# Weighted expert rows, summed by accumulating gathers inside the expert stage of a transformer block

## The chip, the cores and the metric

The kernel runs on one NeuronCore of a Trainium2 chip. The metric is the device time of one execution in microseconds (us). The engines are PE (TensorE, matrix products), DVE (VectorE), ACT (ScalarE), POOL (GpSimd) and SP (SyncE, here only DMA issue); PEld is PE's loading of stationary operands.

## The reference, cut to what matters

One block for x of 4 sequences x 512 tokens x 512 channels: a gate, causal attention with 16 heads, a second gate, and a mixture of experts. This is the part that the change touches:

```python
scores = sigmoid(x @ gate_w)                    # 2048 tokens, 32 experts
# the best 2 of 4 groups are masked out; top 6 experts of the rest
weights = take_along_axis(scores, selected_experts); weights /= sum(weights)
xs = repeat(x, 6)[argsort(selected_experts)]     # rows in expert order
g, u = ragged_dot(xs, w_gate, sizes), ragged_dot(xs, w_up, sizes)    # 512 -> 352
d = ragged_dot(silu(g) * u, w_down, sizes)                          # 352 -> 512
expert_out = sum(d[unsort].reshape(T, 6, 512) * weights[..., None], axis=1)
shared = silu(x @ sw_gate) * (x @ sw_up) @ sw_down                  # 512 -> 704 -> 512
out = x1 + expert_out + shared        # x1: the stream after attention
```

All products are made in three passes over operands that are split into a high and a low part.

## The kernel before

The program is a row of stages, and between stages all engines meet.

`attention` also routes the first three sequences, `choose` on DVE, and POOL sends their rows: `send` takes a tile of 128 rows (`x_rows`), which SP has loaded, and `send_rows` scatters it six times to the HBM tensor `xs` (`slots_in`), one slot for each chosen expert. POOL's order of work (weight splits "u", query splits "r" and "h", sends "z") is written out by hand in `POOL_ORDER`.

`last_route_and_shared_up` does the same for the last sequence and computes the hidden values of the shared expert, `hsh`, in 24 items (6 parts of the weights by 4 sequences). SP loads the shared weights part by part, and stores a block of zeros behind the rows of each expert (`filled`). POOL scatters the last 24 times. DVE makes a table that gives the expert and the first row for each of 127 blocks. 127 is the most that the routing could need; blocks past the last real one read a row of zeros. The table's first column is also used as PE's index of the weights.

`experts` runs 127 blocks of 128 rows in a software pipeline over all engines. For each block ACT loads the rows (`xg`), PE transposes them, ACT and DVE split them, PE multiplies by the expert's gate and up weights, ACT applies SiLU, DVE multiplies, PE transposes the hidden values, ACT and DVE split these, PE multiplies by the down weights, and ACT evicts the result (`rows_out`) and stores it to `ys` (`slots_out`). POOL splits the weights of the 32 experts into high and low, two buffers, so expert e is split when the last gate and up product of expert e - 2 is done. Its last split is expert 31's. At the end SP loads `xT`, 4 MB, the stream x1 transposed.

`combine` is the last stage. SP loads the shared down weights; ACT and DVE split them. For each of 16 tiles of 128 tokens POOL copies six slot numbers and gathers six tiles of rows from `ys`, PE forms the shared product and adds x1 by a product with the identity, and DVE adds the six gathered tiles, each times its weight, to the PSUM result, one after the other. Buffers are double, so POOL waits for DVE's sum of the tile two before. DVE's low part of `hsh` for the next tile stands behind the sums of this tile on its queue.

Of the kernel before, what the change touches and what calls it, by code (L numbers as in the profile page):

```python
# [14 lines left out]
P = 128  # L15
# [18 lines left out]
CAP = T + P  # L34
ZERO_ROW = E * CAP
# [617 lines left out]
def attention(nc, keep, dr, x, fs, wq, wk, wv, wo, gate_w):  # L653
# [5 lines left out]
    with ExitStack() as ctx:  # L659
# [6 lines left out]
        kin, xin = sb("k_rows", [P, TC, P]), sb("x_rows", [P, TC, P])  # L666
# [12 lines left out]
        xc, xh, fc, rowst, rowt = clst, chst, ex, xst, xin  # L679
# [22 lines left out]
        rows_left = sem("rows_left_T")  # L702
# [44 lines left out]
        def _(sp):  # L747
# [111 lines left out]
            def load_rows(u):  # L859
# [7 lines left out]
                sp.dma_start(rowt[:].rearrange("p t c -> p (t c)"), dr["x2"][P * u:P * (u + 1), :]).then_inc(rows_in, 16)  # L867
# [47 lines left out]
        def _(pool):  # L915
# [33 lines left out]
            def send(u, part):  # L949
# [5 lines left out]
                send_rows(nc, pool, dr, rt, slot, rowt[:].rearrange("p t c -> p (t c)"), u, part, 2)  # L955
# [15 lines left out]
            nc.gpsimd.memset(slot[:], 0).then_inc(consts, 1)  # L971
            nc.gpsimd.memset(rt["gm"][:], -1.0).then_inc(consts, 1)
# [28 lines left out]
        def _(pe):  # L1001
            pe.wait_ge(consts, 11)
# [363 lines left out]
        def _(dve):  # L1366
# [139 lines left out]
            for it in range(-1, NIT):  # L1506
                for e in DVE_START if it < 0 else DVE_ORDER[phase(it)]:
                    kind = e[0]
                    if e[0] == "m":
                        if e[1] in "DP":  # L1510
                            b = choice_of(it)
                            if b is not None:
                                if e == "mD0" and b == 0:
                                    dve.wait_ge(consts, 11)
# [48 lines left out]
def last_route_and_shared_up(nc, keep, dr, sw_gate, sw_up, w_gate, w_up, w_down):  # L1563
# [5 lines left out]
    with ExitStack() as ctx:  # L1569
# [4 lines left out]
        x2, rows = sb("x2_last", [P, KC, S]), sb("rows_last", [P, TC, C])  # L1574
        f2 = keep["early"]
# [9 lines left out]
        zero, ends = sb("zero_rows", [P, C]), sb("region_ends", [1, E], I32)  # L1585
# [25 lines left out]
        def _(sp):  # L1611
# [32 lines left out]
            load_shared(3)  # L1644
            sp.wait_ge(ends_done, 1)
# [7 lines left out]
            sp.wait_ge(filled, 16 * (E + 1))  # L1653
# [3 lines left out]
        def _(pool):  # L1657
# [13 lines left out]
            pool.wait_ge(slot_done, B)  # L1671
            for t in range(TC):
                send_rows(nc, pool, dr, rt, slot, rows[:, t, :], NT - TC + t, 0, 1)

        @block.tensor
        def _(pe):
# [17 lines left out]
            for i, (m, b) in enumerate(items):  # L1694
# [12 lines left out]
                if (m, b) == (2, 1):  # L1707
                    pe.wait_ge(row_done, 1)
                    pe.wait_ge(left, KC)
                    for c in range(2):  # L1710
                        last = nc.tensor.transpose(pst[0][0:1, c * P:(c + 1) * P], tabf[:, c:c + 1], ident[:])
                    last.then_inc(row_mm, 1)

        @block.scalar
        def _(act):
# [29 lines left out]
            act.wait_ge(filled, 16 * (E + 1))  # L1745
            act.wait_ge(h_dve, B * (3 - POOL_ITEMS) + 1)
            act.wait_ge(x2_done, CHUNKS + KC)
            for n in range(2):
                row = act.value_load(xrow[0:1, n:n + 1], min_val=0, max_val=ZERO_ROW)
                act.dma_start(f2[:, n, :], dr["xs"][bass.ds(row, P), :]).then_inc(xg_in[n], 16)  # L1750

        @block.vector
        def _(dve):
# [68 lines left out]
            for i in range(B * POOL_ITEMS, len(items)):  # L1822
# [4 lines left out]
                if (m, b) == (3, 0):  # L1827
                    dve.wait_ge(row_mm, 1)
                    then(nc.vector.tensor_copy(ebi[:, 0, :], pst[0][0:1, 0:P]))
# [17 lines left out]
def experts(nc, keep, dr, w_gate, w_up, w_down):  # L1847


    ident, tab, blocks, xT = (keep[k] for k in ("ident", "tab", "blocks", "xT"))  # L1850
    xrow = keep["rowtab"]
    with ExitStack() as ctx:
# [3 lines left out]
        raw, xg = keep["we_raw"], keep["early"]  # L1856
# [428 lines left out]
```

## Time and profile before

| what | value |
|---|---|
| device time, median of 3 runs | 2552.12 us (2549.28 to 2552.67) |
| the profiled execution, its own time | 2533.66 us |
| its span, first to last instruction | 2531.6 us |
| PE busy in the span | 2253.8 us, 89% |
| POOL busy in the span | 1444.6 us, 57% |
| expert stage | about 1456 to 2366 us |
| last stage | about 2366 to 2531.6 us |

All times inside the kernel are us from the start of the profiled span. "Idle before" is the time that an engine stood still ahead of an instruction, and the arrow names what ended it. A busy PE is not PE at its peak, because matmuls are pipelined.

### The profile page before, as it was taken

How to read it: one execution, taken by the hardware profiler on the slowest of the kernel's cores; microseconds unless marked ns; L12 is line 12 of the kernel's file. 1: busy time of each engine (PE TensorE's matmuls, PEld its weight loads, DVE VectorE, ACT ScalarE, POOL GpSimd, SP SyncE). 2: the span in 40 equal slices, each digit the busy share in tenths (PEclk: the TensorE clock that was granted, in tenths of full speed). 3: DMA queues.
4: the chain of work that ended last, by engine and by line, in shares of the span. 5: the costliest groups of instructions: out<-in, count | busy, mean ns of one | idle time of the engine just before them, and what ended most of it. 6: DMA issues, size and time to landing. Idle time of an engine off the chain costs nothing. (4 is left out here: it accounts for less than half of the span.)

```text
span 2531.6 us, 42000 instructions
## 1 busy us (share of the span) xinstructions
PE 2253.8 (89%) x12059; PEld 1928.7 (76%) x12060; DVE 1264.8 (50%) x2120; ACT 1171.2 (46%) x2505; POOL 1444.6 (57%) x976
## 2 busy tenths in 40 slices
PE   1579999999999989898979989999999799999666
PEld 1458888888877768777768689999988699999544
DVE  6737777777755675767653222222222122222365
ACT  3347677777767767776631123333322132333210
POOL 7647777777754556576634046350669955410376
PEclk6789999999999999999979999999999899999888
DMA  4234444433354455554357045352557655522466
GB/s 122 70 114 129 126 125 150 154 100 121 107 169 155 125 163 160 177 175 141 117 220 266 24 138 181 113 166 86 181 163 226 194 169 181 199 86 78 127 196 188
DMA packets 285671, 372.37 MB, mean 147 GB/s; under 512 B 20213, under 2 KB 187193, under 8 KB 280825
## 3 DMA queue, kind: packets, MB, share of 16 engines
q1 hardware_dynamic: 229112, 251.41, 32.2%
q10 hardware_dynamic: 41088, 69.22, 8.4%
q0 software_dynamic: 15360, 50.34, 6.1%
q8 instruction: 60, 0.98, 0.2%
q14 instruction: 51, 0.41, 0.1%
HBM read 257.66 MB, written 113.25 MB: 147 GB/s over the span
## 5 line engine op out<-in xcount | busy, mean ns | idle before, releaser
L1918 POOL TENSOR_SCALAR we_high<-we_raw 128x1408 fp32r<-128x1408 f32 (+1 forms) x95 | 134.1, 1411 | 396.5 <-PE up_e L649 315.9
L1920 POOL TENSOR_TENSOR we_low<-we_raw,we_high 128x1408 fp32r<-128x1408 f32 (+1 forms) x95 | 314.4, 3309 | 7.9
L2034 DVE TENSOR_TENSOR hT_low<-hT_ps,hT_high 128x256 fp32r<-128x256 f32 x127 | 53.9, 425 | 391.4 <-ACT hT_high L1997 391.4
L2047 DVE TENSOR_TENSOR hidden_e<-silu_e,up_e 128x352 f32<-128x352 f32 x127 | 66.1, 521 | 283.6 <-ACT silu_e L2008 283.6
L2008 ACT ACTIVATE silu_e<-gate_e 128x352 f32<-128x352 f32 x127 | 59.0, 465 | 316.8 <-PE up_e L649 316.8
L649 PE MATMUL gate_e<-we_high,xT_high 128*128 x508 | 177.7, 350 | 20.7 <-POOL we_low L1920 20.2
L2013 ACT ACTIVATE rows_out<-down_e 128x512 f32<-128x512 f32 x127 | 75.9, 598 | 216.0 <-PE down_e L649 216.0
L649 PE MATMUL gate_e<-we_high,xT_low 128*128 x508 | 166.1, 327 | 0.0
L649 PE MATMUL gate_e<-we_low,xT_high 128*128 x508 | 165.7, 326 | 0.0
L649 PE MATMUL up_e<-we_high,xT_high 128*128 x508 | 164.4, 324 | 0.0
L649 PE MATMUL up_e<-we_high,xT_low 128*128 x508 | 163.2, 321 | 0.0
L649 PE MATMUL up_e<-we_low,xT_high 128*128 x508 | 163.1, 321 | 0.0
L649 PE MATMUL down_e<-we_high,hT_high 128*128 x381 | 149.6, 393 | 2.4 <-issue 2.4
L1412 DVE TENSOR_TENSOR pT_low<-weights_T,pT_high 128x512 fp32r<-128x512 f32 (+1 forms) x192 | 108.8, 593 | 84.2 <-ACT pT_high L1244 83.8
L649 PE MATMUL down_e<-we_low,hT_high 128*128 x381 | 150.8, 396 | 0.0
L649 PE MATMUL down_e<-we_high,hT_low 128*128 x381 | 150.5, 395 | 0.0
L1226 ACT ACTIVATE prob<-scores,neg_max 128x128 f32<-128x128 f32 (+3 forms) x256 | 131.6, 528 | 39.5 <-DVE neg_max L1397 39.4
L927 POOL TENSOR_TENSOR q_low<-q_raw,q_high 128x512 fp32r<-128x512 f32 x64 | 111.8, 1754 | 54.4 <-ACT q_high L1209 54.3
L1397 DVE TENSOR_REDUCE neg_max<-scores 128x1 f32<-128x128 f32 (+3 forms) x256 | 110.9, 481 | 63.6 <-PE scores L1054 63.1
L923 POOL TENSOR_TENSOR wK_low<-w_ring,wK_high 128x512 fp32r<-128x512 f32 x64 | 88.4, 1388 | 78.0 <-ACT wK_high L1191 77.9
L923 POOL TENSOR_TENSOR wO_low<-w_ring,wO_high 128x512 fp32r<-128x512 f32 x64 | 92.3, 1445 | 60.3 <-ACT wO_high L1191 60.2
L1235 ACT ACTIVATE prob<-prob,row_inv 128x128 f32<-128x128 f32 (+3 forms) x256 | 122.7, 557 | 7.3 <-DVE row_inv L1405 7.3
(341 smaller groups left out, 7332.4 us busy)
## 6 DMA issues: line engine op xcount, KB each, us to landing
rows_early<-slots_in ACTq DMA_DIRECT2D x129, 256.0 KB, 2.7
slots_out<-rows_out ACTq DMA_DIRECT2D x127, 256.0 KB, 2.1
we_raw<-L_ffn_w_gate SPq DMA_DIRECT2D x32, 704.0 KB, 4.6
we_raw<-L_ffn_w_up SPq DMA_DIRECT2D x32, 704.0 KB, 5.0
q_T<-q_out SPq DMA_DIRECT2D x64, 256.0 KB, 2.5
q_raw<-q_T SPq DMA_DIRECT2D x16, 1024.0 KB, 7.7
w_ring<-L_attn_Wk SPq DMA_DIRECT2D x64, 256.0 KB, 3.1
w_ring<-L_attn_Wv SPq DMA_DIRECT2D x64, 256.0 KB, 4.8
```

What stands on the lines that cost most here:

```text
L649: last = nc.tensor.matmul(out, a, b, start=start and i == 0, stop=stop and i == len(terms) - 1)
L923: tt(w_split(*u, 1), ring[:, i % RING, :], w_split(*u, 0).bitcast(F32), ALU.subtract).then_inc(u_lo, 1)
L927: tt(head(ql, n), head_raw(n), head(qh, n).bitcast(F32), ALU.subtract).then_inc(q_lo, 1)
L1226: last = nc.scalar.activation(prob[:, n % 2, P_AT[i]:P_AT[i] + w], pss[x_][:, at:at + w], ACT.Exp, bias=nmax[:, n % 2, i:i + 1], accum_out ...
L1235: last = nc.scalar.activation(w, w, ACT.Copy, scale=rinv[:, n % 2, i:i + 1])
L1397: last = nc.vector.tensor_reduce(nmax[:, n % 2, i:i + 1], pss[x_][:, at:at + (i + 1) * P], AX.X, ALU.max, negate=True)
L1412: tt(ptl[:, at:at + w], pst[(3 * n + x_) % 2][:, 0:w], pth[:, at:at + w].bitcast(F32), ALU.subtract).then_inc(t_lo, 1)
L1918: nc.gpsimd.tensor_scalar(wh[:, p, at:to], raw[:, at:to], 1.0, 1.0, ALU.mult, ALU.mult).then_inc(w_hi, 1)
L1920: nc.gpsimd.tensor_tensor(wl[:, p, at:to], raw[:, at:to], wh[:, p, at:to].bitcast(F32), ALU.subtract).then_inc(w_split, 1)
L2008: nc.scalar.activation(sg[:], psg[:], ACT.Silu).then_inc(s_done, 1)
L2013: nc.scalar.activation(yb[:, p, :], psy[p][:], ACT.Copy).then_inc(y_ev, 1)
L2047: nc.vector.tensor_tensor(hb[:], sg[:], psu[:], ALU.mult).then_inc(h_done, 1)
```

## The change

Rows in `xs` grow from 512 to 528 numbers (`XW`). The 16 new ones (`meta`) hold the token's eight best weights and its six experts. In the expert stage three small DVE operations pick the weight of a row in its block: the six experts are compared with the block's expert (`ebf`, a new table that PE spreads over all partitions), multiplied by the weights and summed. ACT's eviction multiplies by it, so `ys` holds weighted rows. ACT's load of the next rows moves behind SiLU and waits for DVE's use of the old ones.

When the last expert is split and two blocks past the last real one have been evicted, POOL gathers from `ys` into `acc`, one tile of 128 x 512 for each of 16 token tiles: the first choice by a plain gather, the other five by gathers with `compute_op=ALU.add`. Two pairs of groups of four tiles take turns, and a group's next round waits until its round before has landed. The stage ends when all have. SP fills the 31 blocks of `ys` from block 96 on with zeros in the stage before, and loads the shared down weights behind the last split, where it loaded `xT`. The last stage is written out in full, without loops; SP loads x1's tile, PE's work is as before, with four PSUM banks for two, and DVE has one add a tile.

```diff
+                    nc.gpsimd.tensor_copy(rowt[:, C:XW], keep["meta"][:, u, :]).then_inc(rows_ready, 1)
+                    pool.wait_ge(rows_ready, u + 1)
...
+            sp.dma_start(dr["ys"][NREAL * P:NBLK * P, :].rearrange("(n p) c -> p n c", p=P),
+                         zero[:, 0:C].unsqueeze(1).broadcast_to([P, NBLK - NREAL, C])).then_inc(filled, 16)
...
+                    nc.tensor.matmul(pst[1][:, 0:P], tabf[:, 0:1].broadcast_to([P, P]), ident[:], start=True, stop=True).then_inc(row_mm, 1)
...
-            for b in range(B):
-                sp.dma_start(xT[:, b, :, :], dr["x1"][b].rearrange("p (k s) -> p k s", k=KC)).then_inc(x1_in, 16)
-            sp.wait_ge(x1_in, 16 * B)
+            sp.wait_ge(w_split, len(W_PARTS) * (E + 1) + 1)
+            full, tail = (len(SCH) - 1) * P, SCH[-1][1]
+            sp.dma_start(raw[:, 0:(len(SCH) - 1) * C].rearrange("p (k c) -> p k c", c=C),
+                         sw_down[0:full, :].rearrange("(k p) c -> p k c", p=P)).then_inc(sd_in, 16)
+            sp.dma_start(raw[0:tail, (len(SCH) - 1) * C:len(SCH) * C], sw_down[full:, :]).then_inc(sd_in, 16)
...
+            real = pool.value_load(blocks[0:1, E - 1:E], min_val=NREAL, max_val=NBLK)
+            pool.wait_ge(y_ev, real + (CREDIT + 2))
+            pool.sem_inc(pool_steps, 1)
+            for pair in range(2):
+                for k in range(TOPK):
+                    for g in range(2):
+                        if k:
+                            pool.wait_ge(y_in[g], 16 * TC * (TOPK * pair + k))
+                        for t in range(TC * (2 * pair + g), TC * (2 * pair + g + 1)):
+                            more = dict(compute_op=ALU.add) if k else dict()
+                            pool.indirect_dma_start(acc[:, t, :], None, dr["ys"],
+                                                    bass.IndirectOffsetOnAxis(ap=yslot[:, t, k:k + 1], axis=0), **more).then_inc(y_in[g], 16)
...
-                    nc.scalar.activation(yb[:, p, :], psy[p][:], ACT.Copy).then_inc(y_ev, 1)
+                    nc.scalar.activation(yb[:, p, :], psy[p][:], ACT.Copy, scale=wrow[:, q:q + 1]).then_inc(y_ev, 1)
...
+                    nc.vector.tensor_tensor(match[:], xg[:, p, EAT:EAT + TOPK], ebf[:, bass.ds(n, 1)].broadcast_to([P, TOPK]),
+                                            ALU.is_equal).then_inc(m_steps, 1)
+                    nc.vector.tensor_tensor(mine[:], match[:], xg[:, p, WAT:WAT + TOPK], ALU.mult).then_inc(m_steps, 1)
+                    nc.vector.tensor_reduce(wrow[:, q:q + 1], mine[:], AX.X, ALU.add).then_inc(m_done, 1)
...
+                tt(ob[:, n % 2, :], pso[n % 4][:], acc[:, n, :], ALU.add).then_inc(o_done, 1)
```

## Rows read from the trace of the kernel before

**Rows 1.** The page: span, and shares of the chain that ended last.
```profile
span 2531.6 us, 42000 instructions
...
POOL 3%; issue 2%; DMA 1%; DVE 1%; PE 0%; POOLq 0%; ACT 0%; ACTq 0%; SPq 0%; DVEq 0%
```
**Rows 2.** Windows: stretch, length, busy PE, PEld, DVE, ACT, POOL, PEclk, DMA share, GB/s.
```profile
1500.00:2200.00 700.00, 673.27 (x3938) 616.35 (x3937) 171.37 (x395) 206.19 (x492) 408.11 (x174) 0.99 0.51 162
2271.00:2366.00 95.00, 89.01 (x518) 80.98 (x516) 22.60 (x53) 27.82 (x67) 0.00 (x0) 0.98 0.23 75
2366.00:2531.00 165.00, 101.94 (x416) 78.20 (x416) 91.94 (x146) 25.92 (x50) 107.18 (x112) 0.82 0.64 187
```
**Rows 3.** Waits, last stage: us in total, times, longest.
```profile
POOL slot_tile L2104 <- DVEq L2157: 138.8, 1, 138.8
...
PE out_ps L649 <- DVE h_low L2170: 53.1, 14, 18.9
...
DVE acc L2184 <- DMA expert_rows<-slots_out,slot_tile: 50.4, 14, 6.3
```
**Rows 4.** Groups by line, last stage: busy us, mean ns | idle before.
```profile
L2108 POOL DMA_INDIRECT expert_rows<-slots_out,slot_tile x96 | 103.2, 1076 | 37.4 <-issue 23.2 <-POOL slot_tile L2104 13.1 <-DVE out_rows L2184 1.2
...
L2177 DVE TENSOR_SCALAR wts_tile<-wts 128x8 f32 (+1 forms) x16 | 2.6, 165 | 0.0
```
**Rows 5.** Line 2108, the gathers: time to landing.
```profile
DMA to landing us min/median/max: 3.2/3.8/6.8
```
**Rows 6.** POOL's timeline around 2368 us: start, duration [idle before].
```profile
2367.54 1.06 POOL L2108 DMA_INDIRECT expert_rows<-slots_out,slot_tile  x1 [0.90 <-POOL slot_tile L2104]
2368.91 0.96 POOL L2108 DMA_INDIRECT expert_rows<-slots_out,slot_tile  x1 [0.31 <-issue]
```
**Rows 7.** Line 2013, 2269 to 2366 us: the last evictions of the expert stage.
```profile
L2013 ACT ACTIVATE rows_out<-down_e x15: 597/597/602, 2269.7 to 2363.0; 128x512 f32<-128x512 f32 x15
```
**Rows 8.** Timeline of ACT and PE, start of the last stage.
```profile
2374.41 2.34 ACT L2140 ACTIVATE sd_high<-sd_raw 128x2560 fp32r<-128x2560 f32 x1 [10.81 <-DMA sd_raw<-L_ffn_sw_down]
...
2381.78 0.79 PE L649 MATMUL out_ps<-sd_high,h_high 128*128 128x512 f32 x1 [18.87 <-DVE h_low L2170]
...
2388.89 0.50 PE L649 MATMUL out_ps<-sd_high,h_high 128*128 128x512 f32 x1
...
2394.74 0.50 PE L649 MATMUL out_ps<-sd_high,h_high 128*128 128x512 f32 x1 [0.37 <-DVE h_low L2170]
...
2400.47 0.50 PE L649 MATMUL out_ps<-sd_high,h_high 128*128 128x512 f32 x1 [0.25 <-DVE h_low L2170]
```
**Rows 9.** The page's DMA issues: count, KB each, median us to landing.
```profile
rows_early<-slots_in ACTq DMA_DIRECT2D x129, 256.0 KB, 2.7
...
w_ring<-L_attn_Wk SPq DMA_DIRECT2D x64, 256.0 KB, 3.1
```
**Rows 10.** Timeline, DVE's last instruction.
```profile
2528.21 0.75 DVE L2184 SCALAR_TENSOR_TENSOR out_rows<-expert_rows,wts_tile,acc 128x512 f32<-128x512 f32 x1
```
**Rows 11.** DMA, 2366 to 2531 us: POOL's queue (packets, MB, share of 16 engines).
```profile
q0 software_dynamic: 7680, 25.17, 54.0%
```
**Rows 12.** DMA, 1329 to 1397 us: POOL's queue, 24 scatters.
```profile
q0 software_dynamic: 1920, 6.29, 23.2%
```
**Rows 13.** DMA, 2271 to 2366 us: ACT's queue.
```profile
q10 hardware_dynamic: 3888, 7.08, 23.0%
```
**Rows 14.** DVE's timeline in one expert block.
```profile
2258.70 0.68 DVE L2041 TENSOR_TENSOR xT_low<-xT_ps,xT_high 128x512 fp32r<-128x512 f32 x1
2261.36 0.52 DVE L2047 TENSOR_TENSOR hidden_e<-silu_e,up_e 128x352 f32<-128x352 f32 x1 [1.98 <-ACT silu_e L2008]
```
**Rows 15.** Windows, as in rows 2: the fills and scatters before the experts.
```profile
1347.00:1397.00 50.00, 50.00 (x224) 41.29 (x223) 17.06 (x39) 7.28 (x11) 23.15 (x24) 1.00 0.91 340
```
**Rows 16.** ACT's timeline: the split of part 4 of the shared weights.
```profile
1387.68 1.05 ACT L1721 ACTIVATE sw_high<-sw_raw 128x1024 fp32r<-128x1024 f32 x1
```
**Rows 17.** Windows, as in rows 2: attention with the sends.
```profile
920.00:1296.00 376.00, 334.52 (x1753) 275.83 (x1751) 254.49 (x461) 246.38 (x518) 238.34 (x194) 0.95 0.47 153
```

More of the change, by code:

```diff
@@ L34 @@
 CAP = T + P
+XW = C + 16
+WAT, EAT = C, C + 8
+NREAL = T * TOPK // P
 ZERO_ROW = E * CAP
@@ L1844, with experts @@
 W_PARTS = ((0, W_UP, 1), (W_UP, W_DOWN, 1), (W_DOWN, W_N, 2))
-def experts(nc, keep, dr, w_gate, w_up, w_down):
-    ident, tab, blocks, xT = (keep[k] for k in ("ident", "tab", "blocks", "xT"))
+def experts(nc, keep, dr, w_gate, w_up, w_down, sw_down):
+    ident, tab, blocks, acc, ebf, yslot = (keep[k] for k in ("ident", "tab", "blocks", "acc", "ebf", "yslot"))
     xrow = keep["rowtab"]
@@ L2047, in step, with combine @@
                     nc.vector.tensor_tensor(hb[:], sg[:], psu[:], ALU.mult).then_inc(h_done, 1)
-            pipeline(dve, NBLK, 2, 2, step)
-def combine(nc, keep, dr, sw_down, out):
-    xT, ident, hsh, wts, slot = (keep[k] for k in ("xT", "ident", "hsh", "wts", "yslot"))
+            pipeline(dve, NBLK, 4, 2, step)
+def combine(nc, keep, dr, out):
+    ident, hsh, acc = (keep[k] for k in ("ident", "hsh", "acc"))
     NS = len(SCH)
+    tail = SCH[-1][1]
     with ExitStack() as ctx:
@@ L2072, in combine @@
-        pool_steps, act_steps = keep["pool_steps"], keep["act_steps"]
-        block = ctx.enter_context(nc.Block())
-        tail = SCH[-1][1]
-        def loop(eng, step):
-            with eng.Fori(0, B) as b:
-                for t in range(TC):
-                    step(TC * b + t, t % 2, (TC // 2) * b + t // 2, b, t)
+        xc, ob = sb("x1_tile", [P, 2, KC, P]), sb("out_rows", [P, 2, C])
+        pso = [ctx.enter_context(nc.psum_tensor(f"out_ps{i}", [P, S], F32)) for i in range(4)]
+        w_hi, w_lo, hi, lo = sem("sd_hi"), sem("sd_lo"), sem("h_hi6"), sem("h_lo6")
@@ new lines, in load @@
+            def load(n):
+                if n >= 2:
+                    sp.wait_ge(o_mm, n - 1)
+                b, t = divmod(n, TC)
+                sp.dma_start(xc[:, n % 2, :, :], dr["x1"][b].rearrange("p (k s) -> p k s", k=KC)[:, :, at(t)]).then_inc(x_in[n % 2], 16)
+            load(0)
+            load(1)
+            for n in range(NT):
+                if n + 2 < NT:
+                    load(n + 2)
+                b, t = divmod(n, TC)
+                sp.wait_ge(o_done, n + 1)
+                sp.dma_start(out[b, at(t), :], ob[:, n % 2, :]).then_inc(o_out[n % 2], 16)
@@ L2117, in _ @@
+            for p in range(2):
+                sp.wait_ge(o_out[p], 16 * NT // 2)
         @block.tensor
         def _(pe):
-            pe.sem_inc(o_mm, CREDIT)
             pe.wait_ge(w_lo, 1)
-            def step(n, p, half, b, t):
-                pe.wait_ge(lo, done(n))
-                pe.wait_ge(o_done, done(n - 2))
-                parts = [((hh[0:w, p, c, :], hl[0:w, p, c, :]), (wh[0:w, c, :], wl[0:w, c, :])) for c, (at, w) in enumerate(SCH)]
-                split_products(nc, pso[p][:], parts[:1], True, False)
-                pe.wait_ge(x_c, done(n))
+            for n in range(NT):
+                p, bank = n % 2, pso[n % 4]
+                parts = [((hh[0:w, p, c, :], hl[0:w, p, c, :]), (wh[0:w, c, :], wl[0:w, c, :])) for c, (_, w) in enumerate(SCH)]
+                pe.wait_ge(lo, n + 1)
+                if n >= 4:
+                    pe.wait_ge(o_done, n - 3)
+                split_products(nc, bank[:], parts[:1], True, False)
+                pe.wait_ge(x_in[p], 16 * (n // 2 + 1))
@@ L2191, in build @@
+            tt(wl[0:tail, NS - 1, :], raw[0:tail, NS - 1, :], wh[0:tail, NS - 1, :].bitcast(F32), ALU.subtract).then_inc(w_lo, 1)
+            low(0)
+            for n in range(NT):
+                if n + 1 < NT:
+                    low(n + 1)
+                dve.wait_ge(o_mm, n + 1)
+                if n >= 2:
+                    dve.wait_ge(o_out[n % 2], 16 * (n // 2))
+                tt(ob[:, n % 2, :], pso[n % 4][:], acc[:, n, :], ALU.add).then_inc(o_done, 1)
 def build(nc, x, fs, cond, w1, u1, wq, bq, wk, bk, wv, bv, wo, bo, w2, u2,
```

186 lines of the change are left out of this document (74 added, 112 removed).

## Prediction

> **What bounds the kernel now.** I read the page first [rows 1]: the span is 2531.6 us and the chain of waits that ended last names POOL's gathers first, so the end is the last stage's. The windows [rows 2] split the tail. From 1500 to 2200 us, in the expert blocks, PE is busy for 673 of 700 us; the DMA engines are busy 0.51 of that time. From 2271 to 2366 PE is still 89 of 95 us busy, POOL does nothing and the DMA share falls to 0.23. From 2366 to the end PE is busy 102 of 165 us and POOL 107. So the experts are bound by PE and the last stage is not. The waits of the last stage [rows 3] say by what: DVE waits 50.4 us for gathered rows, and DVE's low parts of the hidden values, queued behind those sums, hold PE for 53.1 us. The gathers are 96, of 1.08 us in the mean [rows 4], and one lands 3.8 us after its issue [rows 5]. In POOL's timeline [rows 6] an undisturbed one is 0.96 us behind 0.3 us of issue. The waits [rows 3] also hold what the change wants to use: after its last weight split POOL waits 138.8 us for the end of the expert stage.
>
> Why that gap is there: the expert stage always runs 127 blocks, and the routing of the reference's inputs, counted out, fills 111 of them (it puts expert 29's last block at number 105). Blocks 111 to 126 read a row of zeros. In the new code POOL may start once 113 blocks have left PSUM, which is block 112's eviction. It is the first of the last 15, at 2269.7 us [rows 7].
>
> The sum is made against the profiled execution (2533.7 us of its own time, 2531.6 us of span). The median of the timed runs is 2552.1 us; I carry the difference in us over to it unchanged. 0.2%, about what a measurement here tells from no change, is 5.1 us.
>
> **The change part by part.**
>
> *The last stage* loses its gathers, its weighting and six sums a tile, and the load of its weights, which SP now makes in the expert stage after the last split (2227 us), long before use. It begins with ACT's split of the weights, as before at 2374.4 [rows 8]. Its first product then started 7.4 us later (2381.78); with 0.3 us for the start of the stage, 7.7 us. The first tile took 7.1 us (2381.78 to 2388.89), partly at a low clock. A tile that hardly waited took 2394.74 to 2400.47 less its 0.25 us of waiting, 5.5 us: that is PE's own time, and 15 such are 82 us. DVE, 91.9 us busy in this stage now [rows 2], loses 96 sums of 0.75 us and keeps one add of that size a tile, (91.9 - 72 + 12) / 16 = 2.0 us a tile; ACT has 25.9 / 16 = 1.6 us. Both are under 5.5. The tile of x now comes by its own load of 256 KB, which can start when the tile two before is done, so it has one tile and three products, 6.2 us; a load of 256 KB in weights' rows landed in 3.1 us [rows 9]. After the last product come 0.3 + 0.75 us for the add and 2.6 us for the store, as the old end shows (last DVE instruction over at 2529.0, span 2531.6) [rows 10]. Sum: 7.7 + 7.1 + 82.2 + 3.7 = 100.7 us, against 165.3 us (2366.3 to 2531.6). **Gain 64.6 us.** If the loads of x take 8 us instead of 3.1, each tile waits 1.8 us and 29 us of this go.
>
> *The expert stage* now ends when the last gather has landed. POOL starts at 2270.3 + 0.9 us (the wait between its copy and the first gather [rows 6]) = 2271.2. The old end is 2366.3, so 95 us are covered. There are 16 plain gathers (k = 0) and 80 adding ones. No row shows an adding gather, so it is bounded from both sides, on three resources.
> - POOL's issue. Floor: the plain 0.96 + 0.30 = 1.26 us. Ceiling: twice the descriptor work, 2 x 0.96 + 0.30 = 2.22 us.
> - The DMA engines. A plain gather takes 54.0% of 165 us / 96 = 0.93 us of all 16 [rows 11]; a scatter of the same rows in a crowded stretch 23.2% of 68 us / 24 = 0.66 us [rows 12]. Adding reads the destination too. If every byte counts alike, three passes for two, that is 1.5 times: 1.0 to 1.4 us. If the read side sets the pace, twice: 1.3 to 1.86 us. The blocks that run beside them take 23.0% of 95 us = 21.9 us in all [rows 13].
> - The chain of rounds. Two groups of four tiles take turns, and a group's next round waits for its last to land. Eight issues are 10.1 us, so a landing under 6.3 us costs nothing; the plain one has 3.8 us [rows 5], and the adding one an extra read.
>
> I take 1.5 times on the middle of 0.66 and 0.93, 1.19 us: the engines need 16 x 0.93 + 80 x 1.19 + 21.9 = 132 us. POOL at the last stage's mean of 1.08 + 0.30 = 1.38 us needs 132 us too. The end is 2271.2 + 132 + 3.8 for the last landing + 0.6 for the change of stage = 2407.6 us, 41.3 us later than now. **Loss 41.3 us.** At the floor (1.26 us) it is 2396.6, a loss of 30.3 us.
>
> The trace's plain gather is bound by POOL's issue (1.26 against 0.93 us), and it says nothing on a second read. The Trainium skill, "Collectives: The Full Stack", section "The bandwidth ceiling: the fold count and why AG ≠ RS ≠ AR", states that a DMA that adds needs two source reads on the same read ring, and gives 1.93 as the measured ratio to a copy. By it the DMA sum would be 14.9 + 80 x 1.80 + 21.9 = 181 us and the stage would end some 49 us later than I take; no run here shows it yet.
>
> *The expert blocks.* Each gets three DVE operations on 6 elements. The nearest row is the 128x8 one, 0.16 us [rows 4]; three with their waits are 0.7 us a block. They stand after the low part of x, which ends at 2259.38, and before the hidden product, which begins at 2261.36 after 1.98 us of idling [rows 14]. Cover is left over; without it the cost would be 127 x 0.7 = 89 us. ACT's load of the next rows moves behind SiLU, which ends where the hidden product begins, so to about 2261.5. PE needs the rows two blocks on, about 8 us later, and such a load lands in 2.7 us [rows 9]. Its 0.35 us of issue fit before the next eviction, for which ACT waits for PE. The scale in the eviction is free, the four 1 MB loads of x are gone. Cost 0; rows of 2112 bytes make these transfers 3% longer, hidden too.
>
> *Ahead of the experts.* The fill of 31 blocks of zeros is 31 x 256 KB = 8.1 MB on SP's queue. It goes in at about 1329 us, when the DMA engines have little to do; at the 340 GB/s of the stretch after it [rows 15] it takes 24 us, 9 of them past 1344, where the first expert's weights and 32 fills queue behind it. These ended about 1400 and are needed at 1453. The shared weights of part 4 land about 1368, and 9 us later is still before ACT splits them (1387.7) [rows 16]. The first experts' weights are needed at 1456. Cost 0; if the fill ran at half that rate, part 4 would be about 15 us late and the cost about 15 us. In attention POOL gets 12 copies of 16 columns and a wait each, 0.2 us of copy and up to the 0.9 us of [rows 6] before the next DMA; POOL is busy 238 of 376 us there [rows 17]. Behind them stand q's and the weights' low parts, on which PE waits in turn. Between 0 and 12 us; I take 1.5. PE's one more product and DVE's copy of it: 0.5 us.
>
> **Sum:** -64.6 + 41.3 + 2 = -21.3 us, so 2531 us on the median.
>
> **The rivals.**
> 1. *Adding doubles the DMA time* (slower). Place: the 80 adding gathers. At 2 x 0.93 = 1.86 us the engines need 14.9 + 148.8 + 21.9 = 185.6 us; with about 1 us for the last to land and 0.6, the stage ends at 2458.4, 92.1 us later, and the kernel is 29.5 us slower, 2582 us. It decides from 1.49 us on (2429 us less 2271.2, 1.6, 14.9 and 21.9, over 80), 1.6 times the plain one. For it: an adding read has to be moved by the same engines. Against it: the same bytes took 0.66 us where the engines were crowded, twice of which is 1.3 us. By the Trainium skill's ratio, above, it would be 25 us slower.
> 2. *Adding doubles POOL's issue* (slower). At 2.22 us POOL needs 20.2 + 177.6 = 197.8 us: 107 us later, 44 us slower, 2596 us. It decides from 1.67 us. Against it: scatters and gathers, unlike in direction, cost POOL the same 0.96 us.
> 3. *POOL's floor holds.* 1.26 us each, nothing else binds: 2552 - 32 = 2520 us.
> 4. *Between:* 1.4 to 1.49 us on the engines; within 0.2% or a little faster, about 2546 us.
> 5. *Adding is far dearer* (a row read, summed and written before the next starts, so that a round's landing rules): three issues and a landing make a round, and ten rounds add. At 10 us a landing that is 20 + 138 us and the kernel some 6 us slower, at 20 us a landing 20 + 238 us and over 100 us slower.
>
> **How the numbers follow.** My forecast 0.34 (2522 to 2540 us); floor 0.12; between 0.16 (0.05 of it faster, 0.11 within 0.2%); doubled DMA time 0.18; doubled issue 0.10; far dearer 0.10. Faster 0.51, same 0.11, slower 0.38. The range from 2518 to 2596 us leaves out a little below the floor and most of the last case, 0.12. The likeliest case's own range is 2522 to 2540 us.
>
> **What the profile after would show.** The last stage about 100 us, PE at 5.5 us a tile, no wait for gathers. POOL's first gather about 1 us behind block 112's eviction, near 2271 us, and 96 gathers in 125 to 140 us. The issue and landing of the adding gathers tell rivals 1, 2 and 5 apart: issues of 1.3 us with waits between rounds and a DMA share near 1 are rival 1; issues of 2 us rival 2; long landings at a low share rival 5. Expert blocks still 6.7 us apart. The forecast is wrong if the adding gather is over 1.49 us, if tiles of the last stage wait for x, or if the stages before 1456 us move by more than 3 us.

## The result and the profile after

The changed kernel takes 2585.97 us in the median (2585.0 to 2594.43, 4 runs), the kernel before 2550.7 us beside it (2548.58 to 2552.67, 4 runs): a ratio of 1.0135, 95% interval 1.0112 to 1.0159. It is slower by 35 us, where I had forecast 21 us faster. One thing is needed to read the profiles: in some executions of either kernel ScalarE stands still for 21 to 25 us near 1380 us. The first profile of before is one without that wait, the first of after one with it, so their spans (2531.6 and 2592.7 us) differ by 61 us and not by 35. The experiments have both kinds of both kernels.

The page of the changed kernel (span; busy slices; chain; POOL's gathers with their busy time, mean ns and idle time before):

```profile
span 2592.7 us, 42124 instructions
...
DVE  6737777777765666757552334343455444432012
...
POOL 7657777777754557566612044442479864528820
...
DMA  4234444444444446543387045443456654449942
...
PE 3%; DVE 0%; ACT 0%; issue 0%
...
L1957 POOL DMA_INDIRECT expert_sums<-slots_out,yslot x96 | 138.7, 1444 | 73.6 <-ACT x_batch L2049 44.1
```

The chain that ended last now runs through PE's products of the last stage alone, where POOL's gathers led before [rows 1]. The gathers stand in slices 36 to 39, as POOL's 2, 8, 8, 2 and DMA's 9, 9 show. In windows (the expert blocks, the gathers, the last stage; columns as in rows 2):

```profile
1483.00:2300.00 817.00, 769.39 (x4472) 703.85 (x4473) 355.07 (x787) 245.00 (x558) 445.69 (x190) 0.98 0.50 157
2316.00:2490.00 174.00, 96.81 (x512) 85.81 (x511) 27.29 (x89) 28.47 (x65) 138.15 (x96) 0.80 0.96 185
2493.00:2592.70 99.70, 88.18 (x416) 67.01 (x416) 30.64 (x50) 17.65 (x34) 0.00 (x0) 0.95 0.26 85
```

The last stage takes 99.1 us from ACT's first instruction, and PE is busy 88 of them, against 102 of 165 before [rows 2]. But the stretch ahead of it, in which POOL gathers, has grown to 174 us, and PE is busy for only 97 of them. POOL's timeline where the plain gathers end, and at the last one, with the start of the last stage:

```profile
2315.48 1.05 POOL L1957 DMA_INDIRECT expert_sums<-slots_out,yslot  x1 [44.10 <-ACT x_batch L2049]
2316.84 0.96 POOL L1957 DMA_INDIRECT expert_sums<-slots_out,yslot  x1 [0.30 <-issue]
...
2324.35 0.95 POOL L1957 DMA_INDIRECT expert_sums<-slots_out,yslot  x1 [0.31 <-issue]
2325.61 1.60 POOL L1957 DMA_INDIRECT expert_sums<-slots_out,yslot  x1 [0.30 <-issue]
2327.51 1.56 POOL L1957 DMA_INDIRECT expert_sums<-slots_out,yslot  x1 [0.30 <-issue]
...
2482.07 1.54 POOL L1957 DMA_INDIRECT expert_sums<-slots_out,yslot  x1 [0.30 <-issue]
...
2493.60 2.34 ACT L2161 ACTIVATE sd_high<-we_raw 128x2560 fp32r<-128x2560 f32 x1 [56.36 <-PEq L1865]
```

A plain gather costs POOL 0.95 us and 0.30 of issue, as before [rows 6]. An adding one costs 1.54 and 0.30, from the first one on, with no wait between rounds. From the first start to the end of the last, 168.1 us pass, and 10.0 more until the last stage begins. The DMA of the stretch 2316 to 2490 us:

```profile
q0 software_dynamic: 12800, 25.17, 83.8%
q10 hardware_dynamic: 3818, 7.03, 12.2%
```

POOL's queue takes 0.838 x 174 = 145.8 us of all 16 engines. Less 16 plain gathers at the 0.93 us of [rows 11], that is 1.64 us for an adding one, 1.76 times a plain one. A plain one before was 7680 / 96 = 80 packets; (12800 - 16 x 80) / 80 = 144 are an adding one's. Both the engines and POOL are thus nearly full, and the profile alone doesn't say which binds.

The expert blocks have become slower too. Groups of DVE's instructions by line, 1483 to 2300 us (busy us, mean ns, idle before), and one such block in its timeline with POOL's beside it:

```profile
L2083 DVE TENSOR_TENSOR choice_match<-rows_early,expert_of_block 128x6 f32<-128x6 f32 x113 | 89.5, 792 | 0.0
...
L2086 DVE TENSOR_TENSOR choice_weight<-choice_match,rows_early 128x6 f32<-128x6 f32 x113 | 59.0, 522 | 3.9
L2095 DVE TENSOR_TENSOR hidden_e<-silu_e,up_e 128x352 f32<-128x352 f32 x112 | 58.4, 521 | 110.3 <-ACT silu_e L2040 110.1
```

```profile
2268.45 0.68 DVE L2080 TENSOR_TENSOR xT_low<-xT_ps,xT_high 128x512 fp32r<-128x512 f32 x1
2269.05 2.37 DVE L2083 TENSOR_TENSOR choice_match<-rows_early,expert_of_block 128x6 f32<-128x6 f32 x1
2271.45 0.17 DVE L2086 TENSOR_TENSOR choice_weight<-choice_match,rows_early 128x6 f32<-128x6 f32 x1
2271.74 0.16 DVE L2090 TENSOR_REDUCE row_weight<-choice_weight 128x1 f32<-128x6 f32 x1
2271.91 0.52 DVE L2095 TENSOR_TENSOR hidden_e<-silu_e,up_e 128x352 f32<-128x352 f32 x1
```

```profile
2267.88 3.50 POOL L1938 TENSOR_TENSOR we_low<-we_raw,we_high 128x1536 fp32r<-128x1536 f32 x1
```

Comparing six numbers takes 2.37 us and ends at 2271.42, just after POOL's subtraction, which ends at 2271.38; the hidden product then starts with no idle time, where it had 1.98 us to spare [rows 14]. The same line over two stretches, with its durations in ns (min/median/max): first while POOL splits weights (1483 to 2300 us), then while it only gathers (2316 to 2440).

```profile
L2083 DVE TENSOR_TENSOR choice_match<-rows_early,expert_of_block x113: 151/153/3090, 1489.6 to 2296.6; 128x6 f32<-128x6 f32 x113
...
L2083 DVE TENSOR_TENSOR choice_match<-rows_early,expert_of_block x12: 151/152/156, 2316.9 to 2418.9; 128x6 f32<-128x6 f32 x12
```

### The profile page after: what moved, and what is told of

Same layout as the page of the kernel before. It is cut to its first block and busy times, and to the rows that moved or that the text cites. A ratio compares the mean times of both kernels' runs of the same rounds, so it can differ in the third digit from the quotient of the medians.

```text
span 2592.7 us, 42124 instructions
## 1 busy us (share of the span) xinstructions
PE 2263.3 (87%) x12061; PEld 1933.4 (75%) x12062; DVE 1363.1 (53%) x2406; ACT 1173.6 (45%) x2489; POOL 1477.1 (57%) x974
## 5 line engine op out<-in xcount | busy, mean ns | idle before, releaser
L2049 ACT ACTIVATE x_batch<-down_e,row_weight 128x512 f32<-128x512 f32 x127 | 87.3, 688 | 246.4 <-PE down_e L652 205.3
L1957 POOL DMA_INDIRECT expert_sums<-slots_out,yslot x96 | 138.7, 1444 | 73.6 <-ACT x_batch L2049 44.1
L927 POOL TENSOR_TENSOR wK_low<-w_ring,wK_high 128x512 fp32r<-128x512 f32 x64 | 88.6, 1391 | 79.4 <-ACT wK_high L1198 79.3
```

What stands on the lines that cost most here:

```text
L927: tt(w_split(*u, 1), ring[:, i % RING, :], w_split(*u, 0).bitcast(F32), ALU.subtract).then_inc(u_lo, 1)
L1957: pool.indirect_dma_start(acc[:, t, :], None, dr["ys"], bass.IndirectOffsetOnAxis(ap=yslot[:, t, k:k + 1], axis=0), **more).then_inc(y_in[ ...
L2049: nc.scalar.activation(yb[:, p, :], psy[p][:], ACT.Copy, scale=wrow[:, q:q + 1]).then_inc(y_ev, 1)
```

## The experiments

For all runs I read the same four marks from the timelines: DVE's first hidden product (H), ACT's eviction of block 112 (E), ACT's split of the shared down weights, with which the last stage begins (S), and the end. In the kernel before S lies 8.1 us behind the stage's start, because ACT waits there for its weights [rows 8]. They cut the time into three stretches that answer to three parts of the forecast.

```
kernel             ratio (95% interval)     H        H to E   E to S   S to end  span
before             1                        1469.8   799.9    104.7    157.2     2531.6
j_before_again     1.0010 (0.9995-1.0025)   1496.3   801.0    105.0    158.3     2560.6
after              1.0135 (1.0112-1.0159)   1496.6   817.3    179.7     99.1     2592.7
i_after_again      1.0137 (1.0105-1.0168)   1487.7   818.7    179.2    100.1     2585.7
a_fill_last        1.0141 (1.0120-1.0162)   1472.5   817.5    179.5     99.1     2568.6
k_fill_last_again  (one run)                1492.8   816.3    179.3    99.5     2587.9
d_nocopy           1.0127 (1.0105-1.0150)   1473.6   817.3    179.5     99.2     2569.6
b_plain            0.9966 (0.9955-0.9978)   1471.7   817.4    133.2    100.1     2522.4
c_psum             1.0104 (1.0084-1.0124)   1474.0   803.8    179.1     99.4     2556.3
g_half             1.0127 (1.0103-1.0150)   1492.3   816.4    177.3    100.3    2586.4
f_split            0.9898 (0.9874-0.9922)   1491.8   817.5    111.3    112.9     2533.5
h_split_psum       0.9839 (0.9810-0.9869)   1490.9   803.5    111.0    104.9     2510.3
```

H is where the two kinds of execution part: 1470 to 1474 us without the long wait, 1488 to 1497 with it. Behind H each stretch repeats within 2.5 us between runs of the same code, on whichever chip they ran. The times of a to d were taken on one chip, those of f to i on a second and those of j and k on a third, so kernels of different chips are compared by their ratio to the kernel before, which was timed beside each.

**a_fill_last.** The fill of the spare blocks of `ys` goes behind the 32 fills of padding.

```diff
-            sp.dma_start(dr["ys"][NREAL * P:NBLK * P, :].rearrange("(n p) c -> p n c", p=P),
-                         zero[:, 0:C].unsqueeze(1).broadcast_to([P, NBLK - NREAL, C])).then_inc(filled, 16)
...
                 sp.dma_start(dr["xs"][bass.ds(end, P), :], zero[:]).then_inc(filled, 16)
+            sp.dma_start(dr["ys"][NREAL * P:NBLK * P, :].rearrange("(n p) c -> p n c", p=P),
+                         zero[:, 0:C].unsqueeze(1).broadcast_to([P, NBLK - NREAL, C])).then_inc(filled, 16)
```

> The changed kernel, with one edit: the fill of the 16 blocks of zeros in the table of expert rows, split over SP's queue as one transfer, goes in behind SP's 32 fills of the padding instead of ahead of them. The work is the same. Theory A (the fill fills the DMA engines at 1338 us, ScalarE's instructions for the next part then come late, and SiLU waits 23.5 us at 1387 us): ScalarE's wait at that point shrinks to a few us or moves behind the padding, the stage of the last routing goes from 176 back to about 158 to 162 us, and the time falls by 14 to 18 us to about 2570 us. Rival (the wait comes from the bytes as such, 7.9 MB more wherever they stand): the wait stays within 5 us of 23.5 or moves to the end of the stage, and the time stays within 5 us of 2586 us. Second rival (the wait is for the weights of the shared expert, which queue behind the fill): as theory A in time, but then the releaser named for ScalarE or TensorE at 1365 to 1388 us is one of SP's transfers.

That text calls the fill 16 blocks and 7.9 MB; it is the 31 blocks from 96 on. The ratio stays at 1.014. The long wait is gone from this profile, but it is also absent from those of b, c and d, which have the fill in its old place and were taken beside it. So theory A falls, and with it my reading of the 23.5 us. This run does give a profile of the new code without the wait: 2568.6 us of span against 2531.6.

**d_nocopy.** POOL's 12 copies of the weights and experts are left out; the columns are zeroed once, and these rows carry no weight.

```diff
-                    nc.gpsimd.tensor_copy(rowt[:, C:XW], keep["meta"][:, u, :]).then_inc(rows_ready, 1)
-                    pool.wait_ge(rows_ready, u + 1)
```

> The changed kernel without the 12 copies of weights and experts that POOL makes behind each tile's rows in attention: the columns are zeroed once, so these rows carry no weight (that part of the result is left out). Everything else stays. Theory (each copy with its wait holds POOL and what stands behind it, 9.1 us between 1130 and 1296 us in the two profiles compared): the last routing begins about 1297 instead of 1305 us and the time falls by 5 to 9 us to about 2578 us. Rival (the 9.1 us are variation from run to run of attention, which makes the profiled execution of the kernel before 17 us faster than its own median): the time stays within 3 us of 2586 us, and the start of the last routing stands where the run's own attention puts it. The expert blocks do not notice: their gathered rows differ in the padding columns alone.

H is 1473.6 us, no earlier than the 1471.7 to 1474.0 of the three runs with the copies, and the ratio doesn't part from 1.0135. The rival holds: the copies cost nothing that can be seen, and the 9 us between the first two profiles were variation.

**i_after_again, j_before_again, k_fill_last_again.** The changed kernel and the kernel before, unaltered, and a_fill_last once more.

> The changed kernel again, unaltered, as the measure for the runs beside it on the same chip and to see whether the one long wait of its first profile comes back. Three runs with the fill of zeros in its old place (b_plain, c_psum, d_nocopy) showed no wait of ScalarE at about 1365 to 1388 us, so moving the fill explains nothing. Theory now (that wait of 23.5 us was an event of one execution): SiLU waits under 6 us a time near 1375 us, the last routing takes 158 us, the profiled span is about 2568 to 2572 us where the kernel before takes 2534 us, and the ratio of the times is again 1.013 to 1.015. Rival (it belongs to this kernel and comes in some executions): the wait is there again and the span is 18 us longer.

> The kernel before, unaltered, with a profile. In all five profiles of the changed kernel and its variants taken where the kernel before took about 2551 us, ScalarE's SiLU waits 21 to 25 us in one or two waits between 1375 and 1389 us; in all four taken where it took about 2534 us it doesn't. Theory (the wait comes with the chip or the placement of the program in it, and meets the kernel before too, whose first profile happened to be without it): where the kernel before takes about 2551 us its profile shows such a wait of 10 to 25 us at about 1365 to 1390 us and a span of 2548 to 2552 us; where it takes 2534 us there is none. Rival (only the changed kernel, with its fill of zeros, has the wait, and the kernel before loses its 17 us somewhere else): the span is about 2550 us and no wait over 8 us stands there.

> a_fill_last again, beside the kernel before in the same job. If the kernel before takes about 2551 us here: by the theory that the fill has a share in ScalarE's wait near 1380 us, the waits over 5 us there sum to at least 5 us less than the 21 to 25 us of the changed kernel, or stand later, and the time is under 2580 us; by the rival (the fill has no share) they sum to 20 us or more at the same place and the time is 2584 to 2590 us. If it takes about 2534 us here, there is no such wait and the time is 2568 to 2573 us, as in the first run.

The wait came again in i (21.2 us), so that theory of a single event fell. The one that followed, that it meets the kernel before too, held, though j's span of 2560.6 us lies above the 2548 to 2552 us that were expected (the profiled execution was the longest of ten). Here is ACT's timeline in j_before_again, and under it the same place in the changed kernel's first profile.

```profile
1365.85 0.60 ACT L1740 ACTIVATE silu_g<-gate_ps 128x512 f32<-128x512 f32 x1 [7.58 <-issue]
1389.22 0.60 ACT L1740 ACTIVATE silu_g<-gate_ps 128x512 f32<-128x512 f32 x1 [22.77 <-remote]
```

```profile
1363.65 0.60 ACT L1752 ACTIVATE silu_g<-gate_ps 128x512 f32<-128x512 f32 x1 [4.84 <-issue]
1387.71 0.60 ACT L1752 ACTIVATE silu_g<-gate_ps 128x512 f32<-128x512 f32 x1 [23.46 <-remote]
```

Moved behind the padding in k, the fill leaves 23.4 us of waiting at 1385 us: it has no share. On one chip (a to d) the kernel before took 2534 us and no profile had the wait; on two others it took 2551 to 2552 us and all six had it. Between these chips the median differs by 17 us for the kernel before (2534 to 2551 us) and by 16 for the changed one (2570, a_fill_last, to 2587, i_after_again), so it costs both about the same and explains nothing of the ratio. Compared at equal kind, before to a_fill_last, the change adds 2.7 us ahead of H, 17.6 from H to E and 74.8 from E to S, and takes 58.1 behind S: 37.0 us in all. In the pair with the wait, j_before_again to after, the four are 0.3, 16.3, 74.7 and -59.2: 32.1 us. Either answers to the 35 us that were timed.

**b_plain.** The 80 adding gathers become plain ones, which overwrite: the sums are left out.

```diff
-                            more = dict(compute_op=ALU.add) if k else dict()
+                            more = dict()
```

> The changed kernel with plain gathers: the 80 gathers that add now overwrite, so the sums of six rows are left out and each tile holds its last row only. Bytes written, indices, order and waits stay. Theory (adding costs POOL 1.54 instead of 0.95 us of issue and the DMA engines about 1.64 instead of 0.93 us): issues of 0.95 + 0.30 us, the 96 gathers take about 121 to 130 us of which POOL's issue is the bound, the stretch from the first gather to the start of the last stage falls from 178 to about 128 us, and the time falls by about 48 us to about 2538 us, below the kernel before. Rival 1 (the address lists with a stride of six and the blocks beside them are what is slow, not the adding): the plain ones take over 1.4 us each here too and the time falls by under 20 us. Rival 2 (the waits between rounds rule): POOL waits at each round for the landing and the gain is under 35 us.

The theory holds. E to S falls from 179.5 to 133.2 us, and the time by 44 us against a_fill_last beside it, to 0.34% below the kernel before. The gathers by line, with durations in ns, and what POOL waited for:

```profile
L1957 POOL DMA_INDIRECT expert_sums<-slots_out,yslot x96: 942/947/1058, 2290.7 to 2410.3; - x96
...
  issue: 28.6, 94
  DMA expert_sums<-slots_out,yslot: 1.0, 1
```

All 96 are out in 120.6 us, about 96 x 1.26, and one wait for a landing is 1 us. The rounds, the indices and the blocks beside them are not what is slow. Adding costs 46.3 us here, 0.58 us a gather: close to the difference between 1.54 and 0.95 us.

**g_half.** The adding gathers fetch 256 of 512 columns; the sums of the others are left out.

```diff
-                            pool.indirect_dma_start(acc[:, t, :], None, dr["ys"],
+                            pool.indirect_dma_start(acc[:, t, 0:C // 2] if k else acc[:, t, :], None, dr["ys"],
```

> The changed kernel with the 80 adding gathers cut to the first 256 of 512 columns: the same number of rows and rounds, half the bytes; the sums of the other columns are left out. Theory A (POOL's writing of the descriptors binds: a row to add needs more of them, whatever its length): an issue stays at 1.50 to 1.54 + 0.30 us, the 96 issues take 165 us again, the DMA share of the stretch falls from 0.99 to about 0.6, and only the last landing and the blocks beside it get shorter: 5 to 9 us less than the changed kernel, ratio to the kernel before about 1.010. Theory B (the DMA engines bind and POOL's issue is held up by a full queue): the issue falls toward the plain 0.95 + 0.30 us and the stage ends some 40 us earlier, ratio about 0.998.

It separates the two resources that the profile of after left tied. The first fence is the gathers of g_half with what POOL waited for, the second its windows, the third its DMA from 2310 to 2480 us.

```profile
L1957 POOL DMA_INDIRECT expert_sums<-slots_out,yslot x96: 945/1541/1602, 2310.3 to 2476.5; - x96
...
  issue: 28.9, 95
```

```profile
2311.00:2478.00 167.00, 92.49 (x512) 82.34 (x510) 27.19 (x89) 28.27 (x65) 138.05 (x96) 0.79 0.66 129
```

```profile
q0 software_dynamic: 12800, 14.69, 52.8%
```

Half the bytes and a DMA share of 0.66 instead of 0.96, but the same packets, the same 1.541 us an issue and the same 166 us from first start to last. Theory A holds: POOL's issue binds, and it goes with the adding and its packets, not with the bytes. The forecast of 5 to 9 us saved was too much. From first gather to S it is 175.8 us, against 177.6 us in i.

**c_psum.** The three small operations take one input and their results from a PSUM tile, into which the experts of the blocks are copied once.

```diff
-                    nc.vector.tensor_tensor(match[:], xg[:, p, EAT:EAT + TOPK], ebf[:, bass.ds(n, 1)].broadcast_to([P, TOPK]),
+                    nc.vector.tensor_tensor(psm[:, P:P + TOPK], xg[:, p, EAT:EAT + TOPK], psm[:, bass.ds(n, 1)].broadcast_to([P, TOPK]),
...
-                    nc.vector.tensor_tensor(mine[:], match[:], xg[:, p, WAT:WAT + TOPK], ALU.mult).then_inc(m_steps, 1)
+                    nc.vector.tensor_tensor(psm[:, P + 8:P + 8 + TOPK], psm[:, P:P + TOPK], xg[:, p, WAT:WAT + TOPK], ALU.mult).then_inc(m_steps, 1)
```

> The changed kernel with one edit: the three small DVE operations of a block (compare, product, sum over 6 columns) take one input and their results from a PSUM tile; the list of the blocks' experts is copied there once. Work and waits stay. Theory (compare and product had both inputs in SBUF and are held up to 3 us each by a weight split that GpSimd has under way on the shared port): compare falls from 0.79 us in the mean and product from 0.52 us to about 0.15 us each, no single one over 0.5 us, the blocks up to number 112's eviction take about 814 instead of 832 us, and the time falls by 12 to 18 us to about 2570 us. Rival (three operations in a row with their waits stand in the chain between the low part of x and the hidden product, whatever they read): their times fall but the blocks stay at 832 us within 4 us and the total within 5 us of 2586 us.

In c_psum the two operations are, with durations in ns:

```profile
L2085 DVE TENSOR_TENSOR match_ps<-rows_early,match_ps x127: 152/155/158, 1467.0 to 2363.0; 128x6 f32<-128x6 f32 x127
L2088 DVE TENSOR_TENSOR match_ps<-match_ps,rows_early x127: 172/172/173, 1467.1 to 2363.2; 128x6 f32<-128x6 f32 x127
```

None is held up any more, and H to E falls from 817.4 to 803.8 us, 13.6 of the 17.5 us that the blocks had lost. The rival, that three serial operations are the cost whatever they read, is left with 3 to 4 us at most. The time falls by 9 us against a_fill_last, taken beside it (2560.64 to 2570.02 us, and the single times don't overlap): less than the 12 to 18 us that were expected. The ratios of c and after overlap in their intervals, but f and h below differ by the same edit and are apart.

**f_split.** Tiles 0 to 7 are gathered in the expert stage, tiles 8 to 15 by POOL in the last. There PE gets eight PSUM banks, DVE makes all low parts before the first of the eight late adds, and SP's loads go ahead of the late stores.

```diff
-            for pair in range(2):
+            for pair in range(1):
...
+        @block.gpsimd
+        def _(pool):
+            for k in range(TOPK):
+                for g in range(2):
+                    if k:
+                        pool.wait_ge(y_in[g], 16 * TC * (TOPK + k))
+                    for t in range(TC * (2 + g), TC * (3 + g)):
...
-        pso = [ctx.enter_context(nc.psum_tensor(f"out_ps{i}", [P, S], F32)) for i in range(4)]
+        pso = [ctx.enter_context(nc.psum_tensor(f"out_ps{i}", [P, S], F32)) for i in range(8)]
...
+                if n >= NT // 2:
+                    dve.wait_ge(y_in[n // TC - 2], 16 * TC * TOPK * 2)
```

> The changed kernel with its gathers cut in two halves: tiles 0 to 7 (48 gathers) in the expert stage as before, tiles 8 to 15 (48) by POOL during the last stage, where 8 PSUM tiles let TensorE run ahead and DVE adds the sums of tiles 8 to 15 at the end. The work is the same. Theory (96 gathers of 1.74 us need 167 us, and only some 95 us of expert blocks cover them; a half needs 84 us and fits under either stage): from the first gather to the start of the last stage 100 to 106 us instead of 178, the last stage 102 to 112 us instead of 99, a ratio to the kernel before of 0.983 to 0.990. Rival (the DMA engines, at 1.64 us for each adding gather, 24 us of loads and stores beside them and rounds that wait for their landing, make the last stage 130 us or more): ratio 0.995 or over.

**h_split_psum.** f_split with the edit of c_psum.

> f_split with the PSUM operands of c_psum as well. Theory (the two costs lie in different stretches, the blocks up to number 112 and the gathers behind them, so the gains add): blocks up to the first gather about 806 instead of 819 us, the rest as f_split, 10 to 13 us less than f_split, ratio to the kernel before 0.979 to 0.986. Rival (the time given back in the blocks is lost again at the gathers): within 4 us of f_split.

The split gives 0.9898 and both edits 0.9839 (2512.5 us, where the kernel before took 2551.7 beside it): faster than before by 39 us. E to S falls by 68 us and the last stage grows by 6 to 14. Between f and h, H to E differs by 14.0 us, the 13.6 of c_psum again; so the two costs add. The medians are 16.3 us apart, where 10 to 13 were expected. In the profiled executions the last stage differs too, by 8.0 us, though the edit isn't in it: PE waits there 7.4 us for tiles of x1 in f and 1.1 in h. Why is not known. In windows of h_split_psum, the two stretches that now carry 48 gathers each:

```profile
2296.00:2405.00 109.00, 91.02 (x516) 81.05 (x514) 27.64 (x89) 29.06 (x67) 69.43 (x48) 0.98 0.84 182
2405.00:2510.00 105.00, 89.53 (x416) 66.65 (x416) 30.38 (x50) 17.69 (x34) 73.71 (x48) 0.94 0.92 200
```

POOL's 69 and 74 us of gathers lie inside 109 and 105 us in which PE is busy for 91 and 90. In f_split the last stage came out a little above its forecast (112.9 us, not 102 to 112), and so did the stretch from the first gather to S (109.7 us, not 100 to 106). The last 15 evictions say where the second comes from. In f_split, b_plain and after they are, with durations in ns and the first and last start:

```profile
L2049 ACT ACTIVATE x_batch<-down_e,row_weight x15: 687/687/688, 2309.3 to 2417.2; 128x512 f32<-128x512 f32 x15
```

```profile
L2049 ACT ACTIVATE x_batch<-down_e,row_weight x15: 687/688/690, 2289.1 to 2383.4; 128x512 f32<-128x512 f32 x15
```

```profile
L2049 ACT ACTIVATE x_batch<-down_e,row_weight x15: 687/687/689, 2313.9 to 2436.6; 128x512 f32<-128x512 f32 x15
```

From the first of them to the last it is 93.3 us before [rows 7], 94.3 beside plain gathers and 107.9 beside the 48 of f_split, of which 40 add; POOL's last issue in this stage of f_split is over at 2394.5 us, and the stage ends 3.4 us after the last eviction starts, so there the blocks bind and not the gathers. The adding gathers thus slow the blocks that are to cover them, by about 14 us in f_split; in after it is 29 us, hidden under the longer gathers. The DMA share during f_split's gathers is 0.98; that the blocks' loads and stores come late by it is likely but wasn't tried.

## Why the prediction was wrong

**The adding gather's price** is the step that failed, "POOL at the last stage's mean of 1.08 + 0.30 = 1.38 us needs 132 us too". The bounds were 1.26 and 2.22 us, and from 1.67 us the sign turns. Measured are 1.84 us: 16 x 1.25 + 80 x 1.84 = 167 us instead of 132. I gave POOL the mean of plain gathers, as if adding asked nothing of it, though no row showed an adding one and the ceiling was in the text. Rival 2 named the right place and resource and was given 0.10; its doubling was too dear, for issue and pause together take 1.46 times as long, with 1.8 times the packets. Half-width gathers (g_half) and plain ones (b_plain) show it.

**The same price on the DMA engines** was taken as 1.19 us and is 1.64. That is above the 1.49 us at which rival 1 decides, but it isn't what bound: g_half frees the engines and gains 2 us. Yet the two were level, for the engines' own sum is 14.9 + 80 x 1.64 + 21.2 = 167 us too. By this estimate a cheaper issue alone would have saved little; no run has the one without the other. The Trainium skill, "Collectives: The Full Stack", section "The bandwidth ceiling: the fold count and why AG ≠ RS ≠ AR", gives 1.93 as the measured ratio of AllGather, which copies, to ReduceScatter, which adds. The trace agrees in direction, with 1.76 for the time of an adding gather over a plain one. The section says nothing of the cost of issuing, which bound here.

**The change of stage** was too small. The last landing was taken as 3.8 us and 0.6 for the change, with 0.3 to S; from the end of the last issue (2483.6) to S (2493.6) it is 10.0 us. The landing was right, for all DMA is over by 2487.5. Here is the DMA of after from there to 2493.5 us:

```profile
DMA packets 0, 0.00 MB, mean 0 GB/s; under 512 B 0, under 2 KB 0, under 8 KB 0
```

For some 6 us nothing moves and no engine is busy. b_plain has the same: its last packets are over before 2414 us and S is at 2422.3, so it isn't the adding. What fills this time isn't known. Together it is 5.3 us more than forecast; with 36.1 of issue (168.1 less 132) and 0.1 at the start it is the 41.5 us by which E to S (2407.6 + 0.3 - 2269.7 = 138.2 us forecast, 179.7 measured) was too short.

**The expert blocks** were costed at nothing and cost 16 to 18 us. The sentence "Cover is left over" rested on 0.16 us for an operation, read from a row of the last stage, where POOL splits no weights. Among the splits the comparison takes 0.79 us in the mean and up to 3.09, which is longer than the cover of 1.98 us; the product, 0.52 us in the mean, takes up to 3.24. The Trainium skill, "SBUF — State Buffer", section "SBUF: two separate sides", states that a DVE operation with two SBUF inputs and a GpSimd operation that reads SBUF hold a shared port pair in turn, each for its whole length. By that rule moving one input to PSUM had to end the stretching, and c_psum does: the longest comparison is 158 ns, the longest product 173. Of the rest, 3 to 4 us, I know only that it stays without the stretching. "The scale in the eviction is free" was wrong in its price: the eviction takes 0.69 us instead of 0.60 [rows 7]. No run tells whether that has a share in the rest.

**The last stage** was right: 100.7 us forecast from its start, which is 100.4 from S, and 99.1 us measured from S. So were the costs of the fill and of the copies in attention: 0 and 1.5 us were forecast, and neither a_fill_last nor d_nocopy shows more.

Together, forecast and measured (before to a_fill_last), in us: ahead +2 and +2.7; blocks 0 and +17.6; E to S +33.5 and +74.8; last stage -56.8 and -58.1. The sums are -21.3 and +37.0. Even with the blocks at nothing the kernel would be 19 us slower; with plain prices for adding and the blocks as they are, it would be 9 us faster, as b_plain shows.

## What to carry to other kernels

Work moved under a cover should be sized by the cover: 95 us of idle POOL hold half of 167 us of gathers, and the same gathers halved between two stages win 23 us (f_split, with the reordering of the last stage that goes with it) where all of them in one stage lose 35; the PSUM operands bring the win to 39. Where a price isn't in the trace and decides the sign, let the uncertain factor fall on each resource in turn, the issuing engine too, and don't give one of them the plain price. The duration of a tiny operation is to be read in the stretch in which it will stand, beside the neighbours that it will have there. And what is moved under a cover can stretch the cover itself: the last 15 evictions spread over 108 us beside f_split's gathers, and over 93 without any.

## What the runs showed of the hardware

- An adding indirect gather of 128 rows costs POOL 1.54 + 0.30 us of issue, a plain one 0.95 + 0.30; with half the columns the adding one still costs 1.54 us. On 16 engines a plain one takes 0.93 us, an adding one 1.64 and one of half width 0.94 us ((0.528 x 170 - 14.9) / 80).
- A DVE comparison of 128x6 numbers with both inputs in SBUF took up to 3.09 us beside POOL's splits, and 0.158 us at most with one of them in PSUM.
- In the last 15 blocks the evictions spread over 93.3 us without gathers, 94.3 beside plain ones, and 107.9 (f_split) and 122.7 us (after) beside adding ones.
- Between the last DMA packet of the gathers and the next stage some 6 us passed in after and over 8 in b_plain, with no engine busy.
- ScalarE waited 21 to 25 us near 1380 us, in one or two waits, in all six profiles on two chips (one of the kernel before, five of the changed one and its variants) and in none of four on a third; moving the fill does not change it. In the changed kernel's first profile, which has the wait too, the DMA share was 1.00 from 1364.2 to 1387.7 us. A packet of an instruction queue stands between 1360 and 1385 us, inside the wait, and the next between 1389 and 1391, after its end at 1387.7. That ScalarE's instructions came late would be a guess, and wasn't tried.
